# Attention in query halves and key-tile pairs, projections beside the loop, maxima from the high parts

## The reference, cut to what matters

```python
x = layer_norm(x, ln_m_g, ln_m_b)                  # the context, 6404 rows
lat = layer_norm(latents, ln_l_g, ln_l_b)          # the 1024 tokens
q = lat @ Wq
kv = jnp.concatenate([x, lat], axis=1) @ Wkv       # 7428 keys
k, v = jnp.split(kv, 2, axis=-1)
...
dots = jnp.einsum('bhid,bhjd->bhij', q, k) * scale
attn = jax.nn.softmax(dots, axis=-1)
out = jnp.einsum('bhij,bhjd->bhid', attn, v)
return out.transpose(0, 2, 1, 3).reshape(b, m, heads * dim_head) @ Wout
```

## Time and profile before

| | us |
|---|---|
| median of 3 executions (2881.78 to 2882.93) | 2882.5 |
| span of the profiled execution | 2884.0 |
| PE busy | 2658.8 (92%) |
| DVE busy | 2348.5 (81%) |
| ACT busy | 2271.1 (79%) |
| POOL busy | 55.4 (2%) |

### The profile page before, as it was taken

One profiled execution on the slowest core, in us unless ns is written; L12 is line 12 of the kernel. 1 busy time (PEld: TensorE's weight loads), 2 busy tenths in 40 slices (PEclk: granted clock), 3 DMA queues, 4 the chain that ended last, 5 costly groups with the idle time before them and its releaser, 6 DMA issues. The chain is left out here.

```text
span 2884.0 us, 93692 instructions
## 1 busy us (share of the span) xinstructions
PE 2658.8 (92%) x35639; PEld 1734.1 (60%) x35639; DVE 2348.5 (81%) x3328; ACT 2271.1 (79%) x2645; POOL 55.4 (2%) x95
## 2 busy tenths in 40 slices
PE   2799999999999999999999999999999999959996
PEld 1256665656565656565656566666656566747884
DVE  8789897979797979798888888888979797547864
ACT  4889897979797979797979798988979795426652
POOL 2100000000000000000000000000000000012001
PEclk9999999999999999999999999999999999979998
DMA  2000000000000000000000000000000000060000
GB/s 75 1 2 1 2 1 2 1 2 1 2 1 1 1 1 1 1 2 1 2 1 2 1 2 0 2 1 2 1 2 0 2 1 2 8 169 1 2 2 10
DMA packets 16345, 22.30 MB, mean 8 GB/s; under 512 B 1960, under 2 KB 13808, under 8 KB 15728
## 3 DMA queue, kind: packets, MB, share of 16 engines
q1 hardware_dynamic: 12816, 14.55, 1.7%
q10 hardware_dynamic: 3296, 4.10, 0.5%
HBM read 18.13 MB, written 0.52 MB: 6 GB/s over the span
## 5 line engine op out<-in xcount | busy, mean ns | idle before, releaser
L800 DVE TENSOR_TENSOR att_prob_low<-att_prob 128x1024 f16<-128x1024 f32 (+1 forms) x944 | 1153.7, 1223 | 196.7 <-ACT att_prob L678 195.9
L678 ACT ACTIVATE att_prob<-all_banks 128x1024 f32<-128x1024 f32 (+1 forms) x944 | 966.0, 1025 | 112.8 <-PE all_banks L565 32.6
L672 ACT ACTIVATE att_scores<-all_banks 128x1024 bf16<-128x1024 f32 x768 | 783.2, 1024 | 0.9 <-PE all_banks L495 0.6
L553 PEld LDWEIGHTS all_banks<-att_v,att_prob 128*128 128x128 bf16 x7552 | 538.3, 99 | 117.5 <-issue 16.1
L553 PE MATMUL all_banks<-att_v,att_prob 128*128 (+1 forms) x7552 | 597.7, 193 | 5.1 <-ACT att_prob L678 5.1
L554 PE MATMUL all_banks<-att_v,att_prob 128*128 (+1 forms) x7552 | 598.5, 195 | 0.0
L554 PEld LDWEIGHTS all_banks<-att_v,att_prob 128*128 128x128 bf16 x7552 | 506.0, 98 | 101.6
L535 PE MATMUL all_banks<-att_qc,att_kc 128*128 (+1 forms) x1888 | 562.5, 379 | 0.0
L535 PE MATMUL all_banks<-att_qd,att_kd 128*128 (+1 forms) x1888 | 562.0, 379 | 0.0
L495 PE MATMUL all_banks<-att_kc,att_qc 128*128 (+1 forms) x1792 | 534.3, 380 | 19.0 <-ACT att_scores L672 14.2
L774 DVE TENSOR_TENSOR att_running<-att_running,att_scores 128x1024 bf16<-128x1024 bf16 x768 | 525.9, 685 | 13.9 <-ACT att_scores L672 13.5
(11 more groups left out here) (276 smaller groups left out, 2810.3 us busy)
## 6 DMA issues: line engine op xcount, KB each, us to landing
prep_ctx<-in_ctx SPq DMA_DIRECT2D x5, 640.0 KB, 8.6
later_ctx<-in_ctx SPq DMA_DIRECT2D x1, 3200.0 KB
experts_up<-in_L_ffn_f SPq DMA_DIRECT2D x1, 2048.0 KB, 8.3
prep_wkv<-in_L_xattn_Wkv ACTq DMA_DIRECT2D x1, 1024.0 KB, 12.3
all_X<-in_x SPq DMA_DIRECT2D x1, 512.0 KB, 4.5
prep_wq<-in_L_xattn_Wq ACTq DMA_DIRECT2D x1, 512.0 KB, 14.5
wout_w<-in_L_xattn_Wout SPq DMA_DIRECT2D x1, 512.0 KB, 4.1
out<-all_X SPq DMA_DIRECT2D x2, 256.0 KB, 2.5
```

The costliest lines, as they stand in the source:

```text
L553: pe.matmul(O[:, j // 4, o:o + DH + 1], w, high, start=False, stop=False, skip_group_check=True)
L672: act.activation(o[:, :], banks[:, :, :].rearrange("p a q -> p (a q)"), ACT.Copy).then_inc(max_copied, 1)
L678: act.activation(prob[t % 2][0:n, :], S[t % 2][0:n, :], ACT.Exp, scale=SCALE).then_inc(exp_done, 1)
L800: dve.tensor_tensor(prob_low[t % 2][0:n, :], p, p.bitcast(BF16)[:, 1:2 * TOKENS:2], op=ALU.subtract)\
```

## The change

Only `stage_attention` is rewritten. What it does now:

- A unit of work is one half of the queries (512) by a pair of key tiles, instead of 1024 queries by one tile. A head has 60 units: 29 pairs and the tail for each half (`SIDE` = 30). A unit issues the same 16 + 8 + 4 matmuls of 65, 65 and 512 columns; the attention sums of a half fit into bank 7, and bank 6 (`Y`) is free for projections.
- The projections no longer stand between heads. Eight value groups for the next head go beside units of the first half (`V_AT`), 15 key pieces for the head after next beside units of the second (`K_AT`), all through the one bank `Y`. The queries are projected and the maxima spread at unit 58.
- `max_slot` uses the high parts of the queries alone: instead of two matmuls over 128 rows (high parts of q in rows 0 to 63, low parts below) it issues two over 64 rows, one on rows 0 to 63 and one on rows 64 to 127, into the two banks of `X`.
- Of the seven blocks of a row, three (`COPIED`: 0, 2, 4) are copied by ScalarE and merged by VectorE as before. Four (`DIRECT`: 1, 3, 5, 6) are reduced by VectorE straight out of PSUM (`take_direct`).
- In the units of those four, GpSimd does the `split` of the probabilities in VectorE's place; there are now three buffers for its result, and two conditions more on it: `exp` waits for the split of two units before, and a split for `apply_low` of three units before.
- The loops of 14 tiles are gone; the one loop left has a body of two heads and runs seven times. In the pass over the maxima of head 0, which ran on two pairs of banks in turn, only `X` is used now, and the projections of head 0's values and head 1's keys run beside it.

The diff, cut to its core (the first `head` is GpSimd's, the second TensorE's; `take_direct` and `maxima` are VectorE's):

```diff
+        COPIED = (0, 2, 4)
+        DIRECT = (1, 3, 5, 6)
+        V_AT = (1, 5, 8, 12, 15, 19, 22, 26)
+        K_AT = (1, 3, 5, 6, 8, 10, 12, 15, 17, 19, 20, 22, 24, 26, PAIRS - 1)
+        REST_AT = {PAIRS - 1: (0, 1), PAIRS: (2, 3)}
...
+            def head(b, e):
+                for g in range(UNITS):
+                    if by_pool(g):
+                        pool.wait_ge(exp_done, EXP0 + b * UNITS + g + 1)
+                        pool.wait_ge(low_done, LOW0 + b * UNITS + g - 2)
+                        p = prob[g % NP][:, :]
+                        pool.tensor_tensor(prob_low[g % NL][:, :], p, p.bitcast(BF16)[:, 1:4 * BANK:2],
+                                           op=ALU.subtract).then_inc(split_pool, 1)
...
-            def max_slot(m, j, c, slot, ready, banks=X, lead=0):
...
-                lhs = qc[:, dyn(par), dyn(j * P, P)].rearrange("p a q -> p (a q)")
-                for i in range(2):
-                    rhs = kc[:, dyn(par), (2 * c + i) * BANK:(2 * c + i + 1) * BANK].rearrange("p a q -> p (a q)")
-                    last = pe.matmul(banks[:, i, :], lhs, rhs, start=True, stop=True)
+            def wait_x(m, slot):
...
+                else:
+                    wait_slot_read(pe, m, slot - 1)
+            def max_slot(m, e, slot):
+                j, c = tile_chunk(slot)
+                wait_x(m, slot)
+                for i in range(2):
+                    r = slice((2 * c + i) * BANK, (2 * c + i + 1) * BANK)
+                    last = pe.matmul(X[:, i, :], qq[i * DH:(i + 1) * DH, e, j * P:(j + 1) * P], kc[i * DH:(i + 1) * DH, e, r], start=True, stop=True)
...
+            def head(b, e, with_max, with_keys):
+                for g in range(UNITS):
...
+                    apply_high(b, e, g)
+                    if with_max:
+                        if slot_of(g) is not None:
+                            max_slot(b + 1, 1 - e, slot_of(g))
+                        elif h == 0:
+                            rest_step(b + 1, 1 - e, REST_AT[p][0])
+                    if p:
+                        apply_low(b, e, g - 1)
+                    if p == PAIRS:
+                        apply_low(b, e, g)
...
+                    if with_max and h == 0 and p in V_AT:
+                        project_v(b + 1, V_AT.index(p))
+                    if with_keys and h == 1 and p in K_AT:
+                        project_keys(b, K_AT.index(p))
+                    if with_max and g == LAST - 1:
+                        pe.wait_ge(exp_done, EXP0 + b * UNITS + g + 1)
+                        spread_top(b + 1, 1 - e)
...
+                    if g + 2 < UNITS:
+                        score(b, e, g + 2)
...
+            def take_direct(m, slot):
+                j, c = tile_chunk(slot)
+                dve.wait_ge(max_scored, m * MAX_SLOTS + slot + 1)
+                dve.tensor_reduce(part[:, j, DIRECT.index(c):DIRECT.index(c) + 1], X[:, :, :], axis=AX.XY, op=ALU.max)\
+                   .then_inc(direct_taken, 1)
...
+            def maxima(m, g):
+                slot = slot_of(g)
+                if slot is not None and slot % MAX_CHUNKS in DIRECT:
+                    take_direct(m, slot)
+                if g and slot_of(g - 1) is not None and slot_of(g - 1) % MAX_CHUNKS in COPIED[1:]:
+                    merge(m, slot_of(g - 1))
+                if slot is not None and slot % MAX_CHUNKS == COPIED[-1] + 1:
+                    fold(m, slot // MAX_CHUNKS)
```

More of the change, by code:

```diff
@@ new lines, in apply_low @@
+            def apply_low(b, e, g):
+                wait_split(pe, b, g)
+                for i, t in tiles(g):
+                    for q in range(4):
+                        w = prob_low[g % NL][:, i * BANK + q * P:i * BANK + (q + 1) * P]
+                        o = q * (DH + 1)
+                        last = pe.matmul(O[:, o:o + DH + 1], w, v[:, e, t, 0:DH + 1], start=False, stop=True,
+                                         skip_group_check=True)
+                last.then_inc(low_done, 1)
@@ new lines, in _ @@
+            act.wait_ge(constants, 1)
+            act.activation(warm[:, :], zeros[0:1, 0:1], ACT.Exp).then_inc(exp_done, EXP0)
+            for c in range(K_CHUNKS):
+                copy_keys(0, 0, c, pers.banks[:, c % 4, :])
+            copy_q(0, 0, 0)
+            copy_q(0, 0, 1)
+            for g in range(UNITS):
+                h, p = divmod(g, SIDE)
+                if slot_of(g) is not None and slot_of(g) % MAX_CHUNKS in COPIED:
+                    copy_slot(0, slot_of(g))
+                if h == 0 and p in V_AT:
+                    copy_v(0, 0, V_AT.index(p))
+                if h == 1 and p in K_AT:
+                    copy_keys(1, 1, K_AT.index(p), Y)
```

702 lines of the change are left out of this document (326 added, 376 removed).

## The result

The changed kernel takes 3092.95 us (median of 4 runs, 3090.64 to 3102.87), the kernel before on the same chip 2882.14. The ratio is 1.0739, 95% interval 1.0723 to 1.0756: 7.4% slower. The forecast was 3075, 6.7% slower.

What follows compares the result with a forecast made beforehand. TensorE was taken to bound the loop, with about 31 us a head between loops; after the change, port waits come back. 68 + 133.5 + 14 x 160 + 148 + 101 + 385.5 = 3076, forecast 3075 us, range 2870 to 3190.

Steps and rivals of the forecast that it cites:

- The head, 160: Steady loop: time between placings of the running maxima, 149.2 us before, summed to 161.3 and taken as 160.
- the walk: Steady loop: seven-block row followed through the engines, TensorE waiting 2.1 us for X, up to 3.6 at key pieces.
- The pair, 0.43: Maxima matmuls over 64 rows: halving gains 0.22, changing rows costs 0.10 + 0.09, so 0.43 us as before.
- The rivals at 0.22 and at 0.62: Maxima matmuls: 0.22 us, kernel 2965, chance 0.14; or 0.62, kernel 3185, chance 0.20 shared with slow GpSimd.
- one after the other without a price: Maxima matmuls run in turn, no cost for changing rows: 0.43 us, 3075 in all; chance within the forecast's 0.48.
- `take_direct` free, two-operand instructions not: VectorE beside GpSimd's split: PSUM reductions stay at 1.22 us; split, merge and fold wait for the SBUF port.
- The first pass, 133.5 after the start of the stage: Head 0's maxima through X alone: eight rows 113 us, placed 133.5 after stage start, against 92.4 before.
- The ends: Outside the steady heads: first pass 133.5 us, port-bound last head 101, the head before it 148, after the stage 385.5.
- The sum: Whole kernel: 68 + 133.5 + 14 x 160 + 148 + 101 + 385.5 = 3076 us, forecast as 3075.
- The rival on the other side: Loop: VectorE's splits and merges run beside GpSimd's split; head 146.5 us, kernel 2872, chance 0.06.
- break-even: Steady loop: a head of 147.2 us would leave the kernel's time unchanged.

Runs made afterwards that it cites:

- the 16-column kernel: Changed kernel, but GpSimd's split subtracts only 16 columns and fills the rest of prob_low with zeros, leaving out those low parts; 2897.69 us, ratio 1.0054.

## Why the prediction was right, point by point

- **The head, 160:** 160.9 over the first fourteen, (2462.1 - 209.9) / 14. The mechanism is the one forecast, a merge held by GpSimd's splits, and the 16-column kernel shows what it costs. But the sizes in it were not right each by itself. GpSimd's split takes 1.89, not 2.12, so the merge of block 4 ends at 1.90 after its start instead of 2.7, and TensorE waits 1.02 in the row shown, not 2.1. Key pieces wait three times a head at 2.4, not twice at 3.6: 7.2 a head either way. In all TensorE stands still for 1800 - 1596.6 = 203 us between 500 and 2300, or 18.2 a head, where the walk had 22.7 of waiting (161.3 less 138.6 of TensorE's own work). Against that the walk had no clock: it took all own work at the full one, while at the mean of 0.97 TensorE is busy 142.7 a head. The two errors, 4.5 less and 4.1 more, cancelled. That the head came out within 1 us is in this part luck.
- **The pair, 0.43:** 0.42, and for the reason given: 0.22 at once, 0.10 in, 0.10 out. The rivals at 0.22 and at 0.62 are out, and so is the last one, "one after the other without a price", by the 0.61 against 1.04 at half clock.
- **`take_direct` free, two-operand instructions not:** 1221 throughout, against held merges of 1.90 and splits of 2.22. The other direction of the lock, of which no row of before told, exists: GpSimd's splits last up to 2969 ns.
- **The first pass, 133.5 after the start of the stage:** 142.9 (210.9 - 68). This is the term that was mis-sized, by 9.4, and no single piece of it is to blame. The first pair of maxima and the spreading:

```profile
84.28 0.39 PE L505 MATMUL all_banks<-att_kc,att_qq 64*128 64x512 f16 x2 [2.59 <-DVE att_qc L754]
...
206.48 3.35 PE L523 MATMUL all_banks<-all_ident,att_top 128*64 128x128 f32 x16 [1.13 <-DVE att_top L788]
```

  The first keys and queries take 16.3 for 12.6: their matmuls start 0.43 apart until 72.7, the half clock, and the first pair waits 2.59 for the queries. The eight rows take 116.6 for 113.2 (a copied block 1.73 for 1.65, a direct one 1.93 for 1.85), the rest steps 5.6 for 4.5, spreading and placing 4.4 for 3.2, since spreading takes 3.35 at the half clock and 1.96 in the earlier trace rows. The 0.43 for the pair itself came out (its reader starts 0.65 after it, 118.21 to 118.86, for 0.63), but by luck: the half clock doubles the pair, and the two matmuls at once halve it. With turns on one bank pair TensorE stands still between blocks, and its granted clock is 0.57.
- **The ends:** the last head 98.4 (2611.0 to 2709.4) against 101 forecast, but not for the reason given. It is not bound by the port: in these 98.4 us TensorE is busy 97.0, GpSimd 60.3 and VectorE 42.5. Seven units take TensorE 11.2 us (0.49 + 0.25 + 0.86 each), while GpSimd's four splits and VectorE's three take 4 x 1.89 + 3 x 1.14 = 11.0 in turns; with the 2.12 of the forecast they would have been longer, 11.9. The small error in time hides a wrong limit. The head before it takes 147.9 against 148. After the stage 381.4 against 385.5; where those 4 went was not looked into.
- **The sum:** 68 + 142.9 + 2400.1 + 98.4 + 381.4 = 3090.8, against 68 + 133.5 + 2388 + 101 + 385.5 forecast. The 12 us more in the loop are 14 x 160.9 against 14 x 160.
- **The rival on the other side** (the port does not hold, 2872) describes what the kernel would be without the lock: 2897.69 in the 16-column kernel, with its 146.9 a head beside the 146.5 reckoned. It was right about the price and wrong about the port. The forecast's break-even, 147.2 a head, was a little high: at 146.9 the kernel was still 0.5% slower, mostly since the first pass costs 9 more than reckoned.

## What to carry to other kernels

Before work is given to GpSimd, count what VectorE does at that moment with two SBUF operands: if these are what releases TensorE's banks, 1000 us of work taken over can be worth less than nothing. Where an engine is late in front of a bank, it matters little whether it is held or busy (160.0 and 158.3 a head here). An instruction's place in a queue in front of a bank that is waited for counts for more than the queue's total; and when several waits hide each other, one-at-a-time experiments can understate what their joint removal gives (here +25, -49 and -35 one by one, -188 together). Two 64-row matmuls side by side pay, by these numbers (0.22 gained, 0.20 lost in changing rows), only if the rows are changed less often than around every two of them, or where the clock is low.

## What the runs showed of the hardware

- A TensorE wait of 2.85 us after a full stretch was followed, in some cases, by the half clock for several microseconds (1.00 at 1148, 0.50 until after 1153); the same wait at 1111.67 left it at 1.00. With the key waits down to 1.8 and less the mean of the loop was 0.98 or 0.99 instead of 0.97, though falls still came, as after 2.81 us without a matmul in the 16-column kernel. The kernel before had 0.97 as well.
- A 2016-byte fill on GpSimd (1.78 us) does not disturb VectorE's merge (682), while a split that reads SBUF (1.89) holds it: the merge of 1029.84 ends 0.54 after the split does. The other way round, a split of GpSimd that starts inside one of VectorE's takes 2.32.
- Two 64-row matmuls of 512 columns on the two halves of the array take the time of one (0.22 at the full clock, 0.43 at half), with 0.10 before and 0.10 behind them for changing the rows in use.
